# Adding the cross-attention mask in VectorE's first pass over the scores of a decoder layer

## What is computed

```python
Q = (input_Q @ W_Q); K = (input_K @ W_K); V = (input_V @ W_V)       # 16 heads of 64
scores = einsum('bhqd,bhkd->bhqk', Q, K) / sqrt(64)
scores = where(attn_mask, -1e9, scores)                              # mask: (8, 256, 77)
attn = softmax(scores); context = einsum('bhqk,bhkd->bhqd', attn, V)
out = context.reshape(b, -1, 1024) @ W_O
```

## Time and profile before

| | us |
|---|---|
| median of 3 runs (lowest, highest) | 636.84 (632.3, 644.2) |
| the profiled execution's own time | 640.39 |
| its span, first to last instruction | 638.6 |
| outside the span (640.39 - 638.6) | 1.8 |
| busy PE / DVE / ACT / POOL | 528.9 / 394.3 / 301.3 / 249.0 |
| mean granted TensorE clock, share of full | 0.942 |

### The profile page before, as it was taken

One profiled execution on the slowest core, in us unless ns is written; L12 is line 12 of the kernel. 1 busy time (PEld: TensorE's weight loads), 2 busy tenths in 40 slices (PEclk: granted clock), 3 DMA queues, 4 the chain that ended last, 5 costly groups with the idle time before them and its releaser, 6 DMA issues.

```text
span 638.6 us, 11817 instructions
## 1 busy us (share of the span) xinstructions
PE 528.9 (83%) x4334; PEld 449.0 (70%) x4334; DVE 394.3 (62%) x1093; ACT 301.3 (47%) x484; POOL 249.0 (39%) x317
## 2 busy tenths in 40 slices
PE   2488779877987889889988997899899899957955
PEld 2376666665867767878778776878887687846755
DVE  4657622488867963796388548954983683554332
ACT  2323344432362765166535654663556277426323
POOL 5820021455256355155252526272465016522210
PEclk9779986987797999999999999999999999989969
DMA  5598997966040414051315232325140601111000
GB/s 186 167 233 174 193 216 143 225 218 205 26 100 1 150 34 121 1 160 52 88 49 147 61 83 72 89 60 118 37 112 19 157 22 42 37 41 38 1 16 17
DMA packets 63709, 62.45 MB, mean 98 GB/s; under 512 B 6868, under 2 KB 60804, under 8 KB 63652
## 3 DMA queue, kind: packets, MB, share of 16 engines
q1 hardware_dynamic: 62148, 56.74, 34.8%
q0 software_dynamic: 1504, 4.95, 2.2%
HBM read 38.28 MB, written 23.10 MB: 96 GB/s over the span
## 4 chain that ended last, share of the span: by engine, by line
PE 54%; DVE 23%; ACT 8%; issue 5%; DMA 5%; POOL 3%; SPq 1%; DVEq 0%; ACTq 0%; POOLq 0%
PE banks L798 9%; PE banks L799 8%; PE banks L800 8%; PE banks L958 5%; DVE banks L2382 4%; PE banks L1049 4%; PE banks L1060 4%; PE banks L935 4%; PE banks L1122 2%; DMA x_in<-in_x 2%; PE banks L972 2%; ACT probs L1752 2%; DMA fold_raw<-fold_dram 2%; DVE hid_lo L2337 2%; PE banks L832 1%
## 5 line engine op out<-in xcount | busy, mean ns | idle before, releaser
L2382 DVE CUSTOM_DVE_ANT_0 banks<-banks,causal_qk 128x256 f32<-128x256 f32 (+1 forms) x256 | 84.1, 388 | 13.0 <-PE banks L935 11.2
L582 POOL TENSOR_SCALAR_AFFINE_SELECT probs<-probs 128x256 f32<-128x256 f32 x128 | 52.2, 435 | 70.1 <-ACT probs L1752 70.1
L565 POOL TENSOR_TENSOR work<-work,rc 128x616 f32<-128x616 f32 x32 | 40.5, 1266 | 99.7 <-DVE rc L2482 99.7
L1752 ACT ACTIVATE probs<-banks 128x768 f32<-128x768 f32 x64 | 51.7, 808 | 32.5 <-PE banks L958 31.8
L1720 ACT ACTIVATE work<-banks 77x512 f32<-77x512 f32 (+1 forms) x72 | 43.2, 600 | 48.4 <-PE banks L1049 44.0
L572 POOL TENSOR_TENSOR fold_lo<-fold_raw,fold_hi 128x616 fp32r<-128x616 f32 x32 | 48.6, 1523 | 43.4 <-ACT fold_hi L1720 43.4
L2480 DVE TENSOR_REDUCE sm<-work 128x8 f32<-128x616 f32 x32 | 25.4, 793 | 51.0 <-ACT work L1782 50.9
L935 PE MATMUL banks<-k_stack,q_stack 96*128 96x256 f32 (+1 forms) x256 | 42.0, 288 | 13.0 <-DVE mneg L2382 9.7
L958 PE MATMUL banks<-q_stack,k_stack 100*128 100x128 f32 (+1 forms) x256 | 47.1, 309 | 5.7 <-DMA q_stack<-mnegT 2.7
L935 PEld LDWEIGHTS banks<-k_stack,q_stack 96*128 96x128 f32 x256 | 36.2, 197 | 20.2 <-DVE mneg L2382 11.6
L2337 DVE TENSOR_TENSOR late<-banks,late 128x512 fp32r<-128x512 f32 x40 | 27.4, 684 | 35.0 <-ACT late L1720 35.0
(11 more groups left out here) (190 smaller groups left out, 1574.7 us busy)
## 6 DMA issues: line engine op xcount, KB each, us to landing
fold_raw<-fold_dram SPq DMA_DIRECT2D x32, 308.0 KB, 3.1
fold_dram<-work SPq DMA_DIRECT2D x8, 616.0 KB, 8.5
rot_dram<-rot_s_hi SPq DMA_DIRECT2D x16, 256.0 KB, 3.0
rot_dram<-rot_s_lo SPq DMA_DIRECT2D x16, 256.0 KB, 2.8
q_stack<-rot_dram SPq DMA_DIRECT2D x32, 128.0 KB, 2.7
k_stack<-rot_dram SPq DMA_DIRECT2D x32, 128.0 KB, 3.0
fold_dram<-fold_raw SPq DMA_DIRECT2D x4, 616.0 KB, 6.1
fold_dram<-fold_raw_hi SPq DMA_DIRECT2D x4, 616.0 KB, 8.4
```

The lines of the kernel that those rows point to most:

```text
L582: last = pool.affine_select(out=diagonal, in_=diagonal, compare_op=ALU.is_ge, fill=0.0, base=0, pattern=[[0, 2], [1, P]], channel_multipli ...
L1752: act.activation(probs[:, n:n + 2, :], bank[:, 0:2, P:4 * P], ACT.Exp, scale=SCALE).then_inc(p_ok, 1)
L2382: last = dve.tensor_tensor_reduce(out=held[:, at], in0=held[:, at], in1=bias, scale=-1.0, scalar=HUGE, op0=ALU.add, op1=ALU.min, accum_out ...
```

## The change

The mask is no longer multiplied into the banks. `softmax2` now begins with an addition of the banks and the mask bias into `sc2` (a new semaphore `raw_ok`), then takes the maximum out of `sc2` and subtracts it in place. What waited for `sub_ok` because of the banks (`transpose_b`, `scores2`) waits for `raw_ok`; PE no longer waits for `mask_ok`; the exponential waits for `sub_ok` as before. The wait for the transposes that still read `sc2` of two groups before (`t2_ps`) stands ahead of the addition.

```diff
             def transpose_b(b):
...
-                    pe.wait_ge(sub_ok, 4 * b)
+                    pe.wait_ge(raw_ok, 4 * b)
...
             def scores2(b, g):
                 if g == 0:
                     pe.wait_ge(xbT_lo, b + 1)
-                    pe.wait_ge(mask_ok, b + 1)
                 else:
-                    pe.wait_ge(sub_ok, 4 * b + g)
+                    pe.wait_ge(raw_ok, 4 * b + g)
                 pe.wait_ge(g_lo, 4 * b + g + 1)
                 for q in range(QT):
                     dst = bank[:, 3 + q, 0:GW]
-                    pe.matmul(dst, ident_bf[:], mask_bf[:, q, 0:S2].rearrange("p s -> p () s").broadcast_to([P, GH, S2]),
-                              start=True, stop=False)
                     for k in range(KD):
                         mm = product(dst, both(xbT, slice(None), k, slice(q * P, (q + 1) * P)),
-                                     both(fold, slice(None), k, g % 2), False, k == KD - 1)
+                                     both(fold, slice(None), k, g % 2), k == 0, k == KD - 1)
...
             def mask_bias(b):
                 dve.wait_ge(mask_ld, 16 * (b + 1))
-                dve.wait_ge(s2_ps, 4 * b)
+                dve.wait_ge(raw_ok, 4 * b)
...
             def softmax2(b, g):
                 dve.wait_ge(s2_ps, 4 * b + g + 1)
                 ps = bank[:, 3:5, 0:GW].rearrange("p q (a s) -> p q a s", s=S2)
-                dve.tensor_reduce(mx2[:, r], ps, AX_X, ALU.max).then_inc(mx2_ok, 1)
-                dve.wait_ge(mx2_ok, 4 * b + g + 1)
+                if g == 0:
+                    dve.wait_ge(mask_ok, b + 1)
                 if 4 * b + g >= 2:
                     dve.wait_ge(t2_ps, 2 * (4 * b + g - 1))
-                dve.tensor_tensor(sc2[r], ps, mx2[:, r].rearrange("p q a -> p q a ()").broadcast_to([P, QT, GH, S2]),
+                hidden_keys = mask_bf[:, :, 0:S2].rearrange("p q s -> p q () s").broadcast_to([P, QT, GH, S2])
+                dve.tensor_tensor(sc2[r], ps, hidden_keys, ALU.add).then_inc(raw_ok, 1)
+                dve.wait_ge(raw_ok, 4 * b + g + 1)
+                dve.tensor_reduce(mx2[:, r], sc2[r], AX_X, ALU.max).then_inc(mx2_ok, 1)
+                dve.wait_ge(mx2_ok, 4 * b + g + 1)
+                dve.tensor_tensor(sc2[r], sc2[r], mx2[:, r].rearrange("p q a -> p q a ()").broadcast_to([P, QT, GH, S2]),
                                   ALU.subtract).then_inc(sub_ok, 1)
```

More of the change, by code:

```diff
@@ L218, in decoder_layer @@
         mask_ld, mask_ok, v2_ld = sem("mask_ld"), sem("mask_ok"), sem("v2_ld")
-        s2_ps, mx2_ok, sub_ok, e2_ok = sem("s2_ps"), sem("mx2_ok"), sem("sub_ok"), sem("e2_ok")
+        s2_ps, mx2_ok, sub_ok, e2_ok, raw_ok = (sem(n) for n in ("s2_ps", "mx2_ok", "sub_ok", "e2_ok", "raw_ok"))
         sm2_ok, rc2_ok, nrm_ok = sem("sm2_ok"), sem("rc2_ok"), sem("nrm_ok")
```

## The result

The changed kernel takes 655.92 us, median of 4 runs (651.62 to 658.08); the kernel before 637.07 on the same chip (632.3 to 644.2). The ratio is 1.0305, with a 95% interval of 1.0255 to 1.0355: 19.4 us slower (0.0305 x 637; the two medians alone lie 18.9 apart). The forecast was 640 with a range up to 653, so the time lies outside it.

The account below looks back on a forecast made before the run. No engine alone bounds the kernel: PE sets the pace mostly, DVE for about a quarter. Masks -5.3, additions +7.5 and POOL's hold +1.2 give +3.4 us on the median 636.84, so 640, range 628 to 653.

Parts of the forecast that it names:

- part 2: In softmax2 DVE gets 32 additions of 0.83 us, 26.6 us more busy time, of which +7.5 us was taken.
- 16 of them uncovered: Additions not hidden by ACT's queue before the exponential; they push later DVE work or the softmax itself.
- the bound 14.1 us: Upper limit for the additions in softmax2: 17 x 0.83 us, if each that pushes something pushes the end.
- the nine that lay on the chain that ended last: Nine softmax2 calls on the chain, eight uncovered and one with hid_lo right behind it: 9 x 0.83 = +7.5 us.
- Part 1: PE loses 64 mask matmuls (L1028), 9.1 us of work, at most 7.9 off the chain; -5.3 us taken.
- the chain's 44 pieces: Pieces of the mask matmul L1028 on the chain, 7.9 us together, the most that could come off it.
- Part 5: softmax2's subtraction, now reading two SBUF tensors, is held by POOL: 0.13 us each, +1.2 us taken, at most 10.7.
- Parts 3 and 4: Banks free after one pass instead of two, gain at most 0.6 us, nothing taken; moved waits (t2_ps, mask_ok, raw_ok) cost 0.
- The rival in which VectorE's list takes over: In the stage of the 16 maxima, DVE 93% busy, added passes push the maxima: +16.4 us, 653; chance 0.24.
- PE's wait for `mneg`: Sign that VectorE's list takes over: PE's wait for DVE's maxima (L935 on L2382) up from 9.7 by 5 us or more.

Follow-up runs that it names:

- Mask products kept: The changed kernel with the 64 mask products put back on PE, DVE keeping its three passes: 655.39 us, ratio 1.0371 to the kernel before.

## Why the prediction was wrong

- **The failed step is the price of part 2.** I had counted 26.6 us of added passes, found 16 of them uncovered, and gave the bound 14.1 us. Then I took the nine that lay on the chain that ended last, 7.5 us. The runs say 12.4 us (7.7 to 17.0) for the passes of groups 0 and 1 and 0.7 (-1.0 to 2.4) for the rest, 13.1 in all. They split by group and not by cover. But in the trace of before 14 of the 17 passes of my bound stand in groups 0 and 1 (11.6 us) and three in groups 2 and 3 (2.5), and all nine of the chain stand in groups 0 and 1 (7.5). So the count of uncovered passes came near the price, and the chain's count lies just below the interval. A chain shows who was last in one execution. In the stage of the maxima PE and DVE hand over to each other all the time, and the chain may run through PE at a place where DVE was only a few tenths ahead.
- **Part 1 was mis-sized.** I took -5.3 us for the mask products; beside two passes it was -0.7 (0.9989), beside three it is open ("Mask products kept"). The work on PE was priced well, 9.1 us against 10.7 less busy; but the chain's 44 pieces were not worth their length. What stood close behind them is not found: with DVE relieved as well the whole gain is 3.8 us. The clock was a little lower too (0.938 for 0.946).
- **Part 5 was mis-sized.** I took 1.2 us and bounded it at 10.7; the two runs that differ in it say 9.0. The mean hold was forecast well (0.13 us, measured 912 - 800 = 0.11). But I weighted it by nine calls of the chain, left out that POOL is held as well, and had no term for the granted clock, which was 0.918 on average for 0.946.
- **Parts 3 and 4 are not contradicted**: I had the early release at 0.6 us at most, and the runs, whose intervals overlap, say 3 us or nothing; the moved waits cost nothing that can be seen (the new addition idles 12.9 us, the old maximum 11.8).
- **The rival in which VectorE's list takes over was right**, in mechanism and nearly in size: it gave 653 with a chance of 0.24. It named PE's wait for `mneg` as its sign, which rose by 7.1 us. In its sum the hold was put at 4.3 us where the two runs say 9.0, and it had no term for the clock, so part of its nearness is luck.

The sum as measured: three passes in the banks without mask products +13.2 (1.0208), reading and writing SBUF instead +9.0, the early release -2.9, in all 19.3 for 19.4. It closes by construction, since each term is the distance between two runs' ratios; it is no test of the parts.

## What to carry to other kernels

To price added work on an engine, ask stage by stage whether that engine waits behind the new instruction, and count every uncovered one nearly in full; the chain that ended last tells who was last and not how close the others were. Do not expect a mirror: at this place, where two engines hand over to each other, 16 more passes on VectorE cost 12.4 us, 32 fewer gave 2.0, and 64 products fewer on TensorE 0.7. A pass over scores that is moved from banks to SBUF gets a second SBUF input, and with it POOL as a neighbour.

## What the runs showed that was not expected

TensorE's granted clock was 0.946 on average in 13 runs of the kernel before, 0.918 in 4 of the changed one, and 0.938 when only mask products were left out. Three of the six falls looked at stand at pauses of PE that another engine's list had lengthened (to 1.60, 3.02 and 2.63 us), but behind pauses of 1.85, 1.9 and 2.12 us at the same products the clock stayed up in the execution of the kernel before and fell in that of the changed one. So the pause alone does not decide. PE's busy time is therefore no measure of its work: 64 matmuls fewer, 7.9 us more. And VectorE's and GpSimd's hold on each other cost the kernel 9.0 us (with what came through the clock) at a mean excess of 0.11 to 0.14 us per subtraction.
